# Self-attention with probabilities turned in 32x32 blocks by VectorE, in a decoder-layer kernel

## The reference

```python
qkv = x @ w_qkv                                  # (8,112,256) @ (256,3072)
q, k, v = split(qkv); to heads (8, 16, 112, 64)
sim  = einsum('bhid,bhjd->bhij', q, k) / 8       # 112 x 112 a head
attn = softmax(sim, axis=-1)
out  = einsum('bhij,bhjd->bhid', attn, v)
x = layernorm(x + out.reshape(8, 112, 1024) @ w_out + b_out)
```

## Time and profile before

| | |
|---|---|
| time, median of 3 runs | 433.1 us (432.99 to 433.89) |
| the profiled execution | 433.16 us |
| its span | 431.4 us |
| granted TensorE clock, mean | 0.997 |
| PE busy | 410.7 us, 95% of the span |
| DVE busy | 243.3 us, 56% |
| ACT busy | 193.9 us, 45% |
| POOL busy | 51.0 us, 12% |

### The profile page before, as it was taken

The page is one execution under the profiler, slowest core; times in us unless marked ns, Lnnn a source line. Parts: engine busy times, 40 slices in busy tenths (PEclk is TensorE's granted clock), DMA queues, the critical chain, the costliest instruction groups (busy, mean ns, idle before and its releaser), DMA issues.

```text
span 431.4 us, 8964 instructions
## 1 busy us (share of the span) xinstructions
PE 410.7 (95%) x3128; PEld 296.3 (69%) x3129; DVE 243.3 (56%) x724; ACT 193.9 (45%) x580; POOL 51.0 (12%) x77
## 2 busy tenths in 40 slices
PE   8999999999999979999999999999989999999992
PEld 7767879778796856776776676676665475666661
DVE  1275765747466566666675667666764642244443
ACT  1164362443526446677566666666683101111220
POOL 4010010100101001000010101010100054212222
PEclk9999999999999999999999999999999999999998
DMA  8999000000000013040404040920000013112210
GB/s 246 374 388 260 6 2 2 0 2 2 1 2 0 2 37 147 2 183 2 184 2 183 11 175 7 364 107 2 2 2 2 1 62 98 57 59 65 70 41 27
DMA packets 15242, 34.25 MB, mean 79 GB/s; under 512 B 2382, under 2 KB 9151, under 8 KB 13921
## 3 DMA queue, kind: packets, MB, share of 16 engines
q1 hardware_dynamic: 13952, 30.72, 20.4%
q0 software_dynamic: 1104, 2.76, 1.8%
q10 hardware_dynamic: 144, 0.23, 0.2%
HBM read 27.27 MB, written 6.70 MB: 79 GB/s over the span
## 4 chain that ended last, share of the span: by engine, by line
PE 88%; DVE 5%; ACT 4%; issue 2%; POOL 0%; POOLq 0%; DVEq 0%; ACTq 0%
PE bank L434 11%; PE bank L633 11%; PE bank L448 7%; PE bank L615 6%; PE bank L504 6%; PE bank L809 6%; PE bank L532 5%; PE bank L649 4%; PE bank L899 4%; PE bank L875 4%; PE bank L881 4%; PE bank L526 4%; PE bank L465 3%; PE bank L491 3%; PE bank L821 3%; PE bank L477 3%
## 5 line engine op out<-in xcount | busy, mean ns | idle before, releaser
L1255 DVE CUSTOM_DVE_ANT_0 p<-bank,mask 112x375 f32<-112x375 f32 x128 | 62.6, 544 | 36.5 <-PE bank L615 36.5
L1015 ACT ACTIVATE p<-p,nm 112x375 f32<-112x375 f32 x128 | 74.8, 609 | 2.0 <-DVE nm L1255 2.0
L633 PEld LDWEIGHTS bank<-ident,p 112*125 112x125 f32 x384 | 48.9, 187 | 22.9 <-issue 14.5
L1022 ACT ACTIVATE pT<-bank 125x336 f32<-125x336 f32 x96 | 42.9, 448 | 46.0 <-PE bank L633 46.0
L633 PE MATMUL bank<-ident,p 112*125 112x112 f32 x384 | 58.8, 286 | 1.0
L434 PE MATMUL bank<-x2T,arena 128*128 128x224 f32 x256 | 53.6, 357 | 0.0
L958 ACT ACTIVATE p<-bank,nm 112x112 f32<-112x112 f32 x128 | 43.7, 366 | 18.3 <-DVE nm L1126 18.2
L434 PEld LDWEIGHTS bank<-x2T,arena 128*128 128x128 f32 x256 | 47.0, 192 | 0.6 <-DMA x2T<-in_xT 0.5
L349 POOL TENSOR_TENSOR rstd<-veps,minus_half 128x1 f32<-128x1 f32 x14 | 7.7, 551 | 290.4 <-DVE veps L1152 290.4
L1126 DVE TENSOR_REDUCE nm<-bank 112x4 f32<-112x448 f32 x32 | 19.1, 619 | 24.1 <-PE bank L465 24.1
L615 PE MATMUL bank<-kT,qz 32*112 32x375 f32 x256 | 28.8, 517 | 3.6 <-ACT x2T L984 2.1
(11 more groups left out here) (143 smaller groups left out, 593.0 us busy)
## 6 DMA issues: line engine op xcount, KB each, us to landing
arena<-in_ug SPq DMA_DIRECT2D x8, 1024.0 KB, 5.6
arena<-in_dn SPq DMA_DIRECT2D x8, 512.0 KB, 6.8
mid<-in_ctxT SPq DMA_DIRECT2D x8, 375.0 KB, 3.1
slots_s<-blank SPq DMA_DIRECT2D x14, 128.5 KB, 3.9
arena<-in_wqk SPq DMA_DIRECT2D x7, 256.0 KB, 6.1
slots_x<-blank SPq DMA_DIRECT2D x14, 128.0 KB, 7.2
p<-slots_s SPq DMA_DIRECT2D x9, 128.5 KB, 2.0
kT<-slots_x SPq DMA_DIRECT2D x9, 128.0 KB, 2.1
```

Source lines behind the costliest of these rows:

```text
L633: mm = pe.transpose(PE_T2[r][0:SK, t * S:(t + 1) * S], p2[i % RING][:, t * SK:(t + 1) * SK], ident[0:S, 0:S])
L1015: act.activation(p2[i % RING], p2[i % RING], ACT.Exp, bias=nm2[:, i % H:i % H + 1], scale=-1.0).then_inc(exp2, 1)
L1022: act.activation(pT2[0:SK, i % RING], PE_T2[r][0:SK, 0:KT * S].rearrange("p (k n) -> p k n", k=KT), ACT.Copy).then_inc(pt2_act, 1)
L1255: v.tensor_tensor_reduce(p2[i % RING], PE_S2[r][0:S, 0:S2], bias[:], 1.0, 3e38, ALU.add, ALU.min, accum_out=nm2[:, i % H:i % H + 1]).then_ ...
```

## The change

The probabilities are no longer turned by TensorE. VectorE transposes blocks of 32x32 within each strip of 32 partitions, and the products around it are cut so that this is a whole transpose. Each of the four partition strips holds one head: scores of one group lie as [strip = head, 32 queries] by [query block i, 112 keys], four query blocks (QB) of 32, the last half empty. A group g now is heads 8(g // 2) + 2 strip + g % 2. After the transpose, a strip holds 32 keys of its head for all queries, four key blocks j.

- score1 issues 32 products a pair instead of 8: 64 rows, 32 (or 16) queries, 112 keys, one for each query block, strip and parity.
- project_v1 writes the values in the same form, [strip, 32 keys] by [key block, 256 features]: 16 products of 256 columns a half instead of 2 of 512. It reads all of wv1 in either half, so it waits for both transfers of wv1 in block 0. The columns of wv1 are put in strip order on the host.
- value1 issues 32 products a pair instead of 8: 32 rows, 64 features, 112 queries, the four key blocks summed in PSUM; strips write different banks, 4 to 7. Both pairs lie in the same banks, so the next block's first values wait for both copies, and each evac_o waits for both pairs. Bank 7 is shared with out1's result, in its upper half.
- turn, evac_pt and bank 4's role in them are gone. turn_blocks(g, b), one VectorE instruction of 128x512, stands right behind each normalise. Padding columns are set to zero once by GpSimd.
- TensorE's order: out1 moves behind between1(b, 0); value1(0) stands between between1(b, 3) and between1(b, 4); value1(1) at the end.
- VectorE's order: rowmax 0, rowmax 1, normalise 0, turn_blocks 0, normalise 1, turn_blocks 1, ln1_a, rowmax 2, rowmax 3, ln1_b, the first projection copy, normalise 2, turn_blocks 2, the second, normalise 3, turn_blocks 3, the third and the fourth.
- The small product q_any for the mask goes to bank 2 instead of bank 7, waits for a projection copy, and prep 7, which follows its use, is asked for by project_v1(3, 0) and no longer by out1(0).
- exps, rowmax and normalise work on 128 partitions instead of 112, with the same elements a partition.

```diff
+SQ = 32
+QB = -(-S // SQ)
...
-        bank = [ctx.enter_context(nc.psum_tensor(f"bank{j}", [128, 512], F32)) for j in range(8)]
+        banks = ctx.enter_context(nc.psum_tensor("banks", [128, 8 * 512], F32))
+        bank = [banks[:, j * 512:(j + 1) * 512] for j in range(8)]
...
-        v1 = [carve(INNER)[0:S] for _ in range(2)]
+        v1 = [carve(INNER).rearrange("p (j n) -> p j n", j=QB) for _ in range(2)]
...
-        p1 = [p2_all[0:S, j * G1 * S:(j + 1) * G1 * S].rearrange("p (k n) -> p k n", k=G1) for j in range(4)]
-        pT1 = [pT_all[0:S, j * G1 * S:(j + 1) * G1 * S].rearrange("p (k n) -> p k n", k=G1) for j in range(4)]
+        p1_all = p2_all[:, 0:4 * QB * 128].rearrange("p (g i n) -> p g i n", g=4, i=QB)
+        p1 = [p1_all[:, g] for g in range(4)]
+        pT1 = [pT_all[:, g * QB * 128:(g + 1) * QB * 128].rearrange("p (j n) -> p j n", j=QB) for g in range(4)]
...
-        PE_S1, PE_J1, PE_T1, PE_U1, PE_W1 = bank[0:2], bank[2:4], bank[4], bank[5:7], bank[7]
+        PE_S1, PE_J1, PE_U1, PE_W1 = bank[0:2], bank[2:4], bank[4:8], bank[7][:, 256:512]
+        U1_ALL = banks[:, 4 * 512:8 * 512].rearrange("p (c n) -> p c n", c=STRIPS)
...
-        def head1(g, n):
-
-            return 2 * G1 * (g // 2) + 2 * n + g % 2
+        def block1(j, full=True):
+
+            return SQ if full or (j + 1) * SQ <= S else S - j * SQ
...
+            g.memset(p1_all[:, :, :, S:128], 0.0).then_inc(padded1, 1)
...
             def project_v1(b, c):
+
                 if b == 0:
-                    pe.wait_ge(w_v[c], 16)
+                    for half in range(2):
+                        pe.wait_ge(w_v[half], 16)
                     pe.wait_ge(qk_sb, 7 + c)
                 elif b == 1:
                     pe.wait_ge(v1_sb, c + 1)
                     pe.wait_ge(xT_loaded[1], 16)
                 else:
                     pe.wait_ge(qk_sb, 4 * b + 3 + c)
-                for k in range(KC):
-                    mm = pe.matmul(PE_J1[c][0:S, :], xT[:, b // 2, k, (b % 2) * S:(b % 2 + 1) * S], wv1[:, c, k, :],
-                                   start=(k == 0), stop=(k == KC - 1))
+                if (b, c) == (3, 0):
+                    pe.wait_ge(prep, 7)
+                for j in (2 * c, 2 * c + 1):
+                    m = block1(j, b % 2 == 0)
+                    at = (b % 2) * S + j * SQ
+                    for k in range(KC):
+                        for strip in range(STRIPS):
+                            mm = pe.matmul(PE_J1[c][SQ * strip:SQ * strip + m, (j % 2) * 256:(j % 2) * 256 + 256],
+                                           xT[:, b // 2, k, at:at + m], wv1[:, strip // 2, k, (strip % 2) * 256:(strip % 2) * 256 + 256],
+                                           start=(k == 0), stop=(k == KC - 1))
                 mm.then_inc(v1_pe, 1)
...
                 cols_b = slice((b % 2) * S, (b % 2 + 1) * S)
-                for n in range(G1):
-                    for g in (2 * pair, 2 * pair + 1):
-                        h = head1(g, n)
-                        r = slice(64 * (h % 2), 64 * (h % 2) + 64)
-                        mm = pe.matmul(PE_S1[g % 2][0:S, n * S:(n + 1) * S], qT[b // 2 % 2][r, h // 2, cols_b],
-                                       kT[b // 2 % 2][r, h // 2, cols_b], start=True, stop=True)
-                        if n == G1 - 1:
-                            mm.then_inc(scores1[g], 1)
-
-            def turn(g, b):
-                if b == 0:
-                    pe.wait_ge(consts, 4)
-                pe.wait_ge(norm1, b * 4 + (g + 1))
-                if b * 4 + g >= 1:
-                    pe.wait_ge(pt1, b * 4 + g)
-                for n in range(G1):
-                    mm = pe.transpose(PE_T1[0:S, n * S:(n + 1) * S], p1[g][:, n, :], ident[0:S, 0:S])
-                mm.then_inc(turn1, 1)
+                for i in range(QB):
+                    m = block1(i, b % 2 == 0)
+                    at = (b % 2) * S + i * SQ
+                    for strip in range(STRIPS):
+                        for par in range(2):
+                            r = slice(64 * par, 64 * par + 64)
+                            mm = pe.matmul(PE_S1[par][SQ * strip:SQ * strip + m, i * 128:i * 128 + S],
+                                           qT[b // 2 % 2][r, 4 * pair + strip, at:at + m],
+                                           kT[b // 2 % 2][r, 4 * pair + strip, cols_b], start=True, stop=True)
+                            if (i, strip) == (QB - 1, STRIPS - 1):
+                                mm.then_inc(scores1[2 * pair + par], 1)
 
             def value1(pair, b):
 
-                pe.wait_ge(pt1, b * 4 + (2 * pair + 2))
+                pe.wait_ge(turned1, b * 4 + (2 * pair + 2))
                 if pair == 0:
                     pe.wait_ge(v1_sb, 2 * b + 2)
                 if b >= 1:
-                    pe.wait_ge(ot1[pair], b)
-                for n in range(G1):
-                    for g in (2 * pair, 2 * pair + 1):
-                        h = head1(g, n)
-                        col = (h // 2 % 4) * S
-                        mm = pe.matmul(PE_U1[pair][64 * (h % 2):64 * (h % 2) + 64, col:col + S],
-                                       v1[b % 2][:, h * D1:(h + 1) * D1], pT1[g][:, n, :], start=True, stop=True)
+                    pe.wait_ge(ot1[0], b)
+                    pe.wait_ge(ot1[1], b)
+                if b >= 2:
+                    pe.wait_ge(y1, b - 1)
+                for j in range(QB):
+                    n = block1(j, False)
+                    for par in range(2):
+                        at = (2 * pair + par) * D1
+                        for strip in range(STRIPS):
+                            rows_s = slice(SQ * strip, SQ * strip + n)
+                            mm = pe.matmul(PE_U1[strip][64 * par:64 * par + 64, pair * S:(pair + 1) * S],
+                                           v1[b % 2][rows_s, j, at:at + D1], pT1[2 * pair + par][rows_s, j, 0:S],
+                                           start=(j == 0), stop=(j == QB - 1))
                 mm.then_inc(pv1[pair], 1)
...
             def out1(t):
@@ -497,7 +511,6 @@
                 pe.wait_ge(ot1[0], t + 2)
                 if t == 0:
                     pe.wait_ge(w_loaded["out"], 16)
-                    pe.wait_ge(prep, 7)
                 else:
                     pe.wait_ge(y1, t)
...
                 score1(0, b)
+                between1(b, 0)
                 if b >= 2:
                     out1(b - 2)
-                between1(b, 0)
                 if b < 2:
                     between1(b, 1)
                 score1(1, b)
                 if b >= 2:
                     between1(b, 1)
-                turn(0, b)
                 between1(b, 2)
-                turn(1, b)
                 between1(b, 3)
-                turn(2, b)
+                value1(0, b)
                 between1(b, 4)
-                turn(3, b)
                 between1(b, 5)
-                value1(0, b)
                 value1(1, b)
                 if b == 1:
                     pe.wait_ge(prep, 5)
-                    pe.matmul(PE_W1[:, 0:S], anyw, ident[0:S, 0:S], start=True, stop=True).then_inc(q_any, 1)
+                    pe.wait_ge(qk_sb, 15)
+                    pe.matmul(PE_J1[0][:, 0:S], anyw, ident[0:S, 0:S], start=True, stop=True).then_inc(q_any, 1)
...
                 act.wait_ge(v1_pe, 2 * b + c + 1)
                 if b >= 2:
                     act.wait_ge(pv1[1], b - 1)
-                act.activation(v1[b % 2][:, 512 * c:512 * (c + 1)], PE_J1[c][0:S, :], ACT.Copy).then_inc(v1_sb, 1)
+                act.activation(v1[b % 2][:, 2 * c:2 * c + 2].rearrange("p j n -> p (j n)"), PE_J1[c][:, :], ACT.Copy).then_inc(v1_sb, 1)
 
             def exps(g, b):
                 act.wait_ge(max1, b * 4 + (g + 1))
                 if b >= 1:
-                    act.wait_ge(turn1, b * 4 + (g - 3))
-                for n in range(G1):
-                    h = G1 * g + n
-                    e = act.activation(p1[g][:, n, :], PE_S1[g % 2][0:S, n * S:(n + 1) * S], ACT.Exp,
-                                       bias=nm1[:, h:h + 1], accum_out=rs1[:, h:h + 1])
+                    act.wait_ge(turned1, b * 4 + (g - 3))
+                for i in range(QB):
+                    n = QB * g + i
+                    e = act.activation(p1[g][:, i, 0:S], PE_S1[g % 2][:, i * 128:i * 128 + S], ACT.Exp,
+                                       bias=nm1[:, n:n + 1], accum_out=rs1[:, n:n + 1])
                 e.then_inc(exp1[g], 1)
 
             def evac_o(half, b):
-                act.wait_ge(pv1[half], b + 1)
+                for h in range(2):
+                    act.wait_ge(pv1[h], b + 1)
                 act.activation(oT1[:, 4 * half:4 * half + 4, b * S:(b + 1) * S],
-                               PE_U1[half][:, 0:4 * S].rearrange("p (k n) -> p k n", k=4), ACT.Copy).then_inc(ot1[half], 1)
+                               U1_ALL[:, :, half * S:(half + 1) * S], ACT.Copy).then_inc(ot1[half], 1)
...
```

(70 more changed lines are left out.)

15 lines of the change are left out of this document (8 added, 7 removed).

## The result

| | before | after |
|---|---|---|
| median of the runs | 433.37 us (432.99 to 433.89) | 435.98 us (434.76 to 436.03) |
| span of the profiled execution | 431.4 us | 434.2 us |
| granted TensorE clock, mean | 0.997 | 0.987 |

The ratio is 1.0051, 95% interval [1.0038, 1.0064]: slower by 0.5%. The forecast was 427.3 us; the direction was wrong. The time lies inside the range (424.5 to 437), near its upper end, by luck: that end was drawn for stretched rounds of eight tiles or a dear transpose, of which only 0.2 us a block came.

The account below looks back on a forecast made before the run. TensorE, busy 95% of the span, was taken as the bound. Blocks 2 to 5 -4.76, block 6 -1.1, blocks 0 and 1 -0.5, block 7 +0.5: -5.9 us, from 433.1 to 427.3; range 424.5 to 437.

Parts of the forecast that it names:

- stretched rounds of eight tiles or a dear transpose: Small-tile rounds stretched part of the way, 433 to 440 us, chance 0.05; or VectorE's transpose at 1.15 us, 432.8.
- Eight tiles at once, transpose at 0.70: Scores and values: 64 passes in 8 rounds, 0.77 us a burst, as before; VectorE's 128x512 transpose takes 0.70 us.
- Rivals 1 and 2: 1: at most four tiles at once, 449 us, chance 0.12; 2: dear transpose, 0.09 near no change, 0.03 beyond.
- Blocks 2 to 5, -1.19 each: Steady blocks: 18.56 less 1.56 for turns plus 0.37 for shape changes is 17.37 us; -4.76 for four.
- c = 3: Fourth project_qk/project_k segment, needing ScalarE's copy of project_v1's second half; no wait in blocks 2 to 5, 0.2 us spare.
- The turns: TensorE's four turns of four transposes go: 4 x 0.39 = 1.56 us per block, on the path in blocks 2 to 6.
- the change of tile shape: TensorE: nine shape changes per block instead of five, 0.09 us each, +0.37 us a block.
- Block 6: Shorter segments than blocks 2 to 5, and c = 3 waits 0.1 us: -1.1 us.
- Blocks 0 and 1, -0.25 each: No out1 as cover; group 2's maximum starts at 6.4 us, c = 3 at 9.05 against 8.71; 15.59 against 15.84.
- Block 7, +0.5, no clock effect: ln1_a waits for turn_blocks(1), project_q starts 10.2 us in, value1(1) at 15.35 against 14.81: +0.5 us; no clock term.
- The wait for the keys, "as before" (2.72): Block 7's end: first cross-attention scores come 2.72 us after value1(1) begins, unchanged, the ScalarE copy being free after 1.03 either way.
- rival 3: Gain partly eaten by waits at c = 3 or dearer shape changes with eight tiles: 429 to 431.5 us, chance 0.11.

Follow-up runs that it names:

- together: both_ahead with value1(0) moved right ahead of value1(1) in blocks 2 to 6; 433.58 us.
- both_ahead: The changed kernel with ScalarE's copies (next values' second half in blocks 0 and 1, second turned tile in block 7) ahead of group 2's exponentials; 428.89 us.
- fill_gap: The changed kernel with six matmuls (twelve passes) on zeros put ahead of project_q in block 7; 432.52 us.
- v1_ahead: The changed kernel with ScalarE's copy of the next values' second half ahead of group 2's exponentials in blocks 0 and 1; 432.99 us.
- hold: both_ahead with the transfers of the context and the shared expert held until block 0's first output; 428.62 us.
- x1_ahead: The changed kernel with ScalarE's copy of the second turned tile ahead of group 2's exponentials in block 7; 431.73 us.
- split: The changed kernel with three ScalarE copy orders turned round and, in blocks 2 to 6, both values between the two projections; 427.9 us.

## Why the prediction was wrong, step by step

- **Eight tiles at once, transpose at 0.70:** right (13 to 14 ns a pass; 0.711 us). Rivals 1 and 2 fell. The Trainium skill, "TensorE: Matmul & The Clock Gate", section "Wait — 56ns, not 53.3ns?", gives about 25 ns as the least from start to start. This trace has 13 ns with eight tiles, so here the measurement decides against it.
- **Blocks 2 to 5, -1.19 each:** right in sign and in having no wait at c = 3 (the copy it needs ended 10.57 us into block 3, as worked out), sized double: -0.60. The turns gave back 1.54 (1.56 forecast). The mis-sized term is the change of tile shape: 4 x 0.09 = 0.37 was added, and 0.95 came. From start to start the values take 2.12 against 1.69, the four projections 6.45 against 6.21, both project_v1 0.11 more, out1 0.10 and the scores 0.07. In the values half of the 0.43 is the rounds of 110 ns instead of 96; the rest are dearer changes. together shows 0.33 of it as the price of values in two places. Block 6 missed by the same sort of amount (-0.71 against -1.1).
- **Blocks 0 and 1, -0.25 each:** they became +1.05 and +0.19. The start of c = 3 was right: 9.05 us into the block by the forecast, 8.98 in block 1 (47.12 - 38.14). In block 0 it was 9.84 (31.09 - 21.25), because the maximum of group 2 came at 7.19 instead of 6.4, behind the stand of 0.89, which no step had. The remaining 0.5 in either block is again the changes and the values. That c = 3 needn't wait for exponentials at all wasn't seen: with that order turned round, both_ahead has block 1 in 14.83 us, 1.4 under the kernel before.
- **Block 7, +0.5, no clock effect:** this is the step that failed. The start of project_q was foreseen (10.2 us into the block; 9.96 measured). That it made one idle stretch of 2.7 us where TensorE before had pauses of at most 1.0, and what follows from it, was not. The clock went to 1.2 GHz twice: 0.91 in the block, 0.73 in the 6.34 us behind it. project_q cost 3.01 to the next segment instead of 1.53, the values behind it 1.38 instead of 0.86, out1 1.4 more. With +1.95 in the block and +1.64 behind it this is 3.6 of the 8.7 us of span between forecast (-5.9) and result (+2.9, start row included), and 3.5 by fill_gap, of whose medians 3.3 show in the segments. The Trainium skill, "TensorE: Matmul & The Clock Gate", section "What's actually happening", says that TensorE's full clock is what activity earns, and the low one the default. The trace agrees as far as it goes: both falls stand behind waits, and filling the longer one gave 1.00 from 163 to 169 us.
- **The wait for the keys, "as before" (2.72):** 2.90. That both pairs of values sit in the same banks was in the text, as a matter of the copy's time; that the keys' copies stand behind that copy, and that 1.8 us could be had, was not.

The 8.7 us are block 7 and the piece behind it 3.6, blocks 2 to 5 2.4, block 0 1.3, block 1 0.4, block 6 0.4, and 0.6 of start. So neither named rival won: of rival 3 (gain partly eaten) the half in the steady blocks came, and the rest is an engine order, a clock and a late instruction packet.

## What to carry to other kernels

Where a change adds work ahead of a releaser, walk every in-order engine behind it: here two transposes on VectorE delayed exponentials on ScalarE, and the copy queued behind these, not the transposes, stopped TensorE. Price an idle stretch of TensorE of some us with what the work behind it takes at the low clock as well (3.3 to 3.5 us here behind waits of 2.7 and 1.8), and see whether moving one instruction on another engine closes it. The change was worth having in the end: with three orders on ScalarE turned round it gives 426.4 us, 1.6% under the kernel before, where as made it lost 0.5%.

## What the runs showed of the hardware

- Eight tiles of the array (two row groups by four column groups, or four by two) run at once, a pass of 112 columns starting every 13 to 14 ns.
- TensorE's clock was at 1.2 GHz behind a wait of 2.73 us (0.50 from 153.3 to 155.9 us in the kernel after), and behind one of 1.78 us in after, v1_ahead and hold, but not in x1_ahead and both_ahead with the same wait.
- Short passes can outrun what brings TensorE its instructions: it stands up to 1.6 us with no releaser at a fixed place of the program and goes on 1.25 to 1.6 us after a packet of 16 KB of the instruction queue has landed (19 stands of 19, also at a DMA share of 0.01). The packet itself took 0.9 to 1.25 us in these cases. With long passes between the values and the scores no stand came (split). Why the packets start when they do isn't shown.
- VectorE turns 128x512 fp32 in 32x32 blocks in 0.711 us from SBUF to SBUF.
